# The first head group's weight columns split ahead of the rest, x loaded first, and item 0 waiting for its own copy

## What is computed

```python
q, kv = ln(x), ln(ctx)
qp, kp, vp = q @ Wq.T + bq, kv @ Wk.T + bk, kv @ Wv.T + bv
s = einsum(qh, kh) / sqrt(32) - scale[h] * dist(query_xy, token_xy) + offset[h]
s = where(token_mask, s, -inf)
x = x + (softmax(s) @ vh) @ Wo.T + bo
x = x + gelu(ln(x) @ W1.T + b1) @ W2.T + b2          # hidden width 2048
```

## Time and the profile before

| | |
|---|---|
| median of 3 runs | 1211.11 us (1210.51 to 1212.82) |
| the profiled execution | 1213.1 us, its span 1211.3 us |
| PE busy | 1189.5 us, 98% |
| POOL, DVE, ACT busy | 949.7, 908.5, 863.5 us |
| mean DMA rate | 193 GB/s |

### The profile page before, as it was taken

The page is one execution under the profiler, slowest core; times in us unless marked ns, Lnnn a source line. Parts: engine busy times, 40 slices in busy tenths (PEclk is TensorE's granted clock), DMA queues, the critical chain, the costliest instruction groups (busy, mean ns, idle before and its releaser), DMA issues.

```text
span 1211.3 us, 27819 instructions
## 1 busy us (share of the span) xinstructions
PE 1189.5 (98%) x9671; PEld 810.5 (67%) x9671; DVE 908.5 (75%) x2474; ACT 863.5 (71%) x1960; POOL 949.7 (78%) x1194
## 2 busy tenths in 40 slices
PE   7899999999999999999999999999999999999999
PEld 4466666667676766767676666767676676766666
DVE  6788868887787878778797887778787877668222
ACT  4699796868778786877778686877778687756332
POOL 5598988788798878889798878879787887758221
PEclk9899999999999999999999999999999999999999
DMA  8567768989799898989889897979988897867553
GB/s 256 168 174 220 176 166 185 212 175 235 179 213 211 188 212 190 222 172 236 196 189 214 194 211 177 233 178 201 222 185 213 191 217 159 190 168 171 148 149 104
DMA packets 434524, 233.23 MB, mean 193 GB/s; under 512 B 349888, under 2 KB 374864, under 8 KB 434384
## 3 DMA queue, kind: packets, MB, share of 16 engines
q1 hardware_dynamic: 434384, 231.45, 83.3%
HBM read 109.66 MB, written 12.58 MB: 101 GB/s over the span
## 4 chain that ended last, share of the span: by engine, by line
PE 88%; POOL 3%; DVE 3%; ACT 2%; issue 1%; SPq 1%; DMA 1%; DVEq 0%; POOLq 0%; ACTq 0%
PE ps_up L883 27%; PE ps_down L903 26%; PE ps_qk L790 12%; PE ps_vo L812 6%; PE ps_s L827 5%; PE ps_pv L868 3%; PE ps_pv L815 3%; PE ps_vo L815 3%; POOL soft L1592 1%; POOL soft L1611 1%; PE ps_down L931 1%; DVE soft L1372 1%; ACT soft L1071 0%; DMA xT<-x_nat 0%; PE ps_down L839 0%
## 5 line engine op out<-in xcount | busy, mean ns | idle before, releaser
L883 PE MATMUL ps_up<-hT,w 128*128 128x256 f16 x3072 | 377.0, 273 | 0.0
L1372 DVE CUSTOM_DVE_ANT_0 soft<-ps_s,soft,factor 128x256 f32<-128x256 f32 x512 | 226.1, 478 | 196.2 <-PE ps_s L827 196.2
L1071 ACT ACTIVATE soft<-soft,neg_max 128x256 f32<-128x256 f32 x512 | 255.7, 501 | 164.8 <-DVE neg_max L1372 163.6
L903 PE MATMUL ps_down<-w,hid 128*128 128x512 f16 x1476 | 359.6, 378 | 0.1
L883 PEld LDWEIGHTS ps_up<-hT,w 128*128 128x128 f16 x3072 | 300.6, 98 | 85.9
L1602 POOL TENSOR_SCALAR p_nat<-soft,row_inv 128x256 f16<-128x256 f32 x448 | 265.3, 603 | 71.2 <-DVE row_inv L1385 68.4
L1611 POOL TENSOR_SCALAR soft<-dist,scale_neg,offset 128x512 f32<-128x512 f32 x256 | 267.0, 1043 | 16.3 <-DVE p_nat L1391 15.4
L1391 DVE SCALAR_TENSOR_TENSOR p_nat<-soft,row_inv,p_nat 128x256 f16<-128x256 f32 x448 | 266.9, 635 | 0.8 <-POOL p_nat L1602 0.8
L1114 ACT ACTIVATE u<-ps_up,bias,up_scale 128x256 f32<-128x256 f32 x256 | 142.5, 557 | 127.1 <-PE ps_up L883 124.1
L903 PEld LDWEIGHTS ps_down<-w,hid 128*128 128x128 f16 x1476 | 141.6, 97 | 125.8 <-DVE x L1445 2.8
L1619 POOL TENSOR_SCALAR hid<-u,hid_scale 128x1024 f16<-128x1024 f32 x63 | 73.2, 1162 | 47.3 <-ACT u L1120 47.3
(11 more groups left out here) (166 smaller groups left out, 1548.4 us busy)
## 6 DMA issues: line engine op xcount, KB each, us to landing
w<-x_scratch SPq DMA_DIRECT2D x252, 256.0 KB, 3.1
stack<-qk_parts SPq DMA_DIRECT2D x256, 96.0 KB
raw<-in_ctx SPq DMA_DIRECT2D x32, 256.0 KB, 3.6
raw<-in_x SPq DMA_DIRECT2D x32, 256.0 KB, 4.2
c_stage<-in_w SPq DMA_DIRECT2D x16, 512.0 KB, 5.4
x<-in_x SPq DMA_DIRECT2D x32, 256.0 KB, 3.6
out<-x SPq DMA_DIRECT2D x31, 256.0 KB, 3.3
tok_rows<-in_tok_xy SPq DMA_DIRECT2D x16, 256.0 KB, 3.7
```

What stands on the lines that cost most here:

```text
L883: mm = e.matmul(ps_up[s % 2][:, 0:L], w_1_sb[:, wp, k, m * P:(m + 1) * P], hT[:, b % 2, :, xp * KT + k, :], start=(k, wp, xp) == (0, 0, 0) ...
L903: mm = e.matmul(ps_down[tt][:], left, w_2_sb[:, s % W2_RING, wp, :], start=first, stop=last)
L1071: e.activation(soft[:, ring, lc, :], soft[:, ring, lc, :], ACT.Exp, scale=-1.0, bias=neg_max[:, ring, lc:lc + 1], accum_out=row_sum[:, rin ...
L1372: e.tensor_tensor_reduce(soft[:, ring, lc, :], ps_s[:, lc * T:(lc + 1) * T], soft[:, ring, lc, :], factor[:, 0:1], 3.0e38, ALU.add, ALU.mi ...
```

## The change

It changes the order of the opening and of the first slots.

- x tiles 0 and 1 are loaded right behind ctx, ahead of W_k. They get a buffer of their own (`x_first`, in the place of `pT`), and ScalarE makes the high halves of all four tiles of batch 0 (`first_x_hi`).
- The small loads, tok_rows of batch 0 and W_v are issued by ScalarE.
- The first 128 columns of W_k and W_q (head group 0) are split first, by ScalarE and VectorE (`weight_hi_first`, `weight_lo_first`), and the projections of group 0 wait for each quarter of those alone. The other 384 columns are split by GpSimd and VectorE (`weight_hi_rest`, `weight_lo_rest`). Group 0's queries use the bank `ps_vo`, so they do not wait for the keys' low half.
- `keep_mask` comes after both halves of chunk 0, and both groups' mask rows follow it at once, ahead of the copies. Item 0 waits for its own copy and mask row (`s_head0`), items 1 to 3 for the other copies.
- W_v is split in slots 0 and 1, its bias matmuls are in slot 0, W_o's halves move from slots 1 and 2 to 2 and 3, W_1's and W_2's each two slots later. The Gram matmuls of W_o and of chunk 0 go from slot -2 to -1 and 1. Group 1 is projected in slots -2 and 0 (before -3 and -1), its copies are in slot 2 (before 1), batch 0's first value projection is in slot 2 (before 0), and `value_bias_out` is in slot 5 (before 4). The warming matmuls of slots -8 and -6 are 2 and 2 rather than 8 and 6.

```diff
@@ lists
-        CHUNK_AT = ((-6, -4), (-2, 0), (2, 4), (6, 8), (10, 12), (14, 16), (17, 19), (20, 22))
-        GRAM = (-31, -29, -6, -2, -2) + (2, 6, 10, 14, 18, 21, 24)
+        CHUNK_AT = ((-13, -12), (0, 2), (4, 6), (8, 10), (11, 13), (15, 17), (18, 20), (21, 23))
+        GRAM = (-31, -29, -4, -1, 1, 4, 8, 12, 16, 19, 22, 25)
...
-            return DMA * (HPG * (G // STACK_RING + 1) + G // HG + 1)
+            return DMA * (HPG * (G // STACK_RING + 1) + G // HG + 1 - (0 if G % STACK_RING else 2))
+        def qk_at(slot, first):
+            yield from (G for G in due(slot, first, GROUP, N_HG) if G != 1)
+            if slot == first + GROUP + 1:
+                yield 1
@@ SyncE
-                    e.dma_start(dst, src).then_inc(s_stack[ring], DMA)
+                    e.dma_start(dst, src).then_inc(s_head0 if G == 0 and j == 0 else s_stack[ring], DMA)
...
+            def mask_copy(G):
+                b, ring = G // HG, G % STACK_RING
+                gate.wait_ge(s_mkept, DMA)
+                src = mask_kept[b:b + 1, :].rearrange("p (o t) -> p o t", o=1).to_broadcast([1, HPG, T])
+                e.dma_start(stack[96:97, ring, :, 1 - query_side(G), :], src).then_inc(s_head0 if G == 0 else s_stack[ring], DMA)
...
-                for sec, at_slot in ((SEC_V, -25), (SEC_O, -14)):
+                for sec, at_slot in ((SEC_O, -14),):
...
-                if slot == -4:
+                if slot == -11:
                     keep_mask()
+                if slot == -10:
+                    for ring in range(STACK_RING):
+                        mask_copy(ring)
@@ TensorE
-                        gate.wait_ge(s_wlo, AT[sec] + 1)
+                        if G > 0:
+                            gate.wait_ge(s_wlo, AT[sec] + 1)
                         for k in range(KT):
+                            if G == 0:
+                                gate.wait_ge(s_wpart[sec], k + 1)
...
-                gate.wait_ge(s_stack[ring], n_stack(i // 4))
+                gate.wait_ge(*((s_head0, 2 * DMA) if i == 0 else (s_stack[ring], n_stack(i // 4))))
...
-                for at_slot, count in ((-30, 1), (-28, 1), (-8, 8), (-6, 6)):
+                for at_slot, count in ((-30, 1), (-28, 1), (-8, 2), (-6, 2)):
...
-                for sec, at_slot in ((SEC_K, -31), (SEC_Q, -29), (SEC_V, -3)):
+                for sec, at_slot in ((SEC_K, -29), (SEC_Q, -27), (SEC_V, 0)):
                     if slot == at_slot:
                         weight_bias(sec)
@@ ScalarE
+                if slot == -32:
+                    load_small()
+                for n in range(4):
+                    if slot == -30 + n:
+                        first_x_hi(n)
+                if slot == -27:
+                    load_value_weight()
...
-                for sec, at_slot in ((SEC_K, -25), (SEC_Q, -20), (SEC_V, -3)):
+                for sec, at_slot in ((SEC_K, -26), (SEC_Q, -20)):
                     if slot == at_slot:
-                        weight_hi(sec, range(KT))
-                for half_of in due(slot, 1, ITEM, 2):
+                        weight_hi_first(sec)
+                for half_of in due(slot, 0, ITEM, 2):
+                    weight_hi(SEC_V, range(2 * half_of, 2 * half_of + 2))
+                for half_of in due(slot, 2, ITEM, 2):
                     weight_hi(SEC_O, range(2 * half_of, 2 * half_of + 2))
-                if slot == -6:
+                if slot == -4:
                     dist_sqrt(0)
@@ VectorE
+            def weight_lo_first(sec, pieces):
+                for k in pieces:
+                    gate.wait_ge(s_fhi, KT * AT[sec] + k + 1)
+                    e.scalar_tensor_tensor(out=w_sec[sec][:, LO, k, 0:P], in0=w_stage[sec][:, k, 0:P], scalar=gain[:, sec, k:k + 1],
+                                           in1=w_sec[sec][:, HI, k, 0:P], op0=ALU.mult, op1=ALU.subtract).then_inc(s_wpart[sec])
...
+                for sec, pieces, at_slot in ((SEC_K, range(3), -6), (SEC_K, range(3, KT), -5), (SEC_Q, range(KT), -3)):
+                    if slot == at_slot:
+                        weight_lo_rest(sec, pieces)
@@ GpSimd
+            def weight_hi_rest(sec):
+                gate.wait_ge(s_gs, GAINED_Q if sec == SEC_Q else GS[AT[sec]])
+                for k in range(KT):
+                    e.tensor_scalar(w_sec[sec][:, HI, k, P:D], w_stage[sec][:, k, P:D], gain[:, sec, k:k + 1], 1.0, ALU.mult, ALU.mult).then_inc(s_rhi)
...
+                for sec, at_slot in ((SEC_K, -23), (SEC_Q, -21)):
+                    if slot == at_slot:
+                        weight_hi_rest(sec)
```

187 lines of the change are left out of this document (103 added, 84 removed).

## The result

The changed kernel took 1217.8 us, median of 4 runs (1217.15 to 1218.32), beside 1210.81 us for the kernel before (4 runs, 1210.25 to 1212.82): ratio 1.005, 95% interval 1.0038 to 1.0062. It is slower, by about 6 us, where I had forecast 1210.9 and a range up to 1214.2. The profiled execution took 1217.54 us with a span of 1215.5.

A forecast was written before the change was run, and what follows sets the result against it. TensorE was taken to bound the kernel, so the total moves with the first MLP matmul's start. First score -3.4, moved work +3.2, waits 0 gave -0.2 us: 1210.9 us, range 1205.8 to 1214.2.

The forecast's parts named there:

- term 1: Opening up to the first score: it comes at 30.9 us, 3.4 us sooner, with bounds 29.7 to 33.5.
- (d): Opening: keep_mask, issued on SyncE behind W_o and chunk 0, waits for them and lands at 27.2 us.
- (e): From keep_mask's landing to the first score: two mask copies, 1.4 us, then head 0's copy, 2.3 us.
- first rival: Opening: mask not held up, arithmetic decides; first score 8.3 us sooner at 26, total 1206 us; chance 0.22.
- step (c): Opening: W_v, W_o and chunk 0 load without a gap in 8.4 us, ending at 26.95.
- Step (a): Opening: small loads and tok_rows delay W_q's last quarter 0.8 us, to 13.35; W_k lands 1.4 to 2.2 us later.
- the opening gains nothing: Opening: transposes slowed beside W_v, or a copy of 3.74 us; first score 33.5, total 1213.5 us; chance 0.08.
- Term 2: Behind the first score: work moved there from the opening adds 3.2 us of TensorE time; waits cost the same.
- some 2 us: Slot 4: VectorE's 5 us of work makes score 6 wait this long, against 1.97 us ahead of score 4 before.
- TensorE's slot 0 has 5.6 us of work and covers it: Slots 0 and 1: VectorE ends slot 1 about 9.4 us after the first score, TensorE asks at 11.5.
- VectorE becomes the bound: Slots 0 to 5: two stalls of 2 us and a clock's fall of 1.7, +3.7, total 1214.6 us; chance 0.14.
- Slots 6 to 28 take other than 78.9 us: Sign that would prove the forecast wrong: the stretch up to the first MLP matmul departing from 78.9 us.

The follow-up runs named there:

- e2: Changed kernel with chunk 0 of W_1 loaded behind group 0's copies, so keep_mask has only W_o ahead of it; 1215.86 us, ratio 1.0031.
- e17: Kernel before with W_v asked for behind all of x's transposes; 1218.14 us, ratio 1.0053.
- e3: Changed kernel with the small loads and tok_rows on SyncE behind W_q and dist_square of part 0 two slots later; 1216.83 us, ratio 1.0043.
- e10: e5 with W_v asked for by SyncE behind the four transposes of x, ahead of W_o; 1213.45 us, ratio 1.001.
- e6: As e5, but four small loads (52 KB) left on ScalarE's queue, only tok_rows on SyncE; 1215.3 us, ratio 1.003.
- e5: Changed kernel with the edits of e2 and e3 together, q_neg's negation and dist_square five slots later than in e3; 1216.12 us, ratio 1.0035.
- e1: Kernel before run once more, no edit; 1212.09 us, ratio 0.9995.
- e12: Kernel before with only item 0's own copy wait and group 0's mask row copied ahead of the other copies; 1211.87 us, ratio 0.9997.
- e16: Kernel before with 18 more filler matmuls, 6 in each of slots 0, 1 and 2; 1213.67 us, ratio 1.0013.
- e18: Kernel before with the edits of e12 and e17 together; 1218.72 us, ratio 1.0056.
- e7: e5 with 2 fillers in place of 13 in slot 0; 1216.11 us, ratio 1.0035.
- e15: e14 with 2 fillers in place of 13 in slot 0; 1212.02 us, ratio 1.0001.
- e9: e7 with K's and Q's halves ahead of the exponentials and W_v's halves in slots 0 and 1; 1215.88 us, ratio 1.0025.
- e13: e10 with chunk 0 asked for behind the two ctx tiles of batch 1; 1213.78 us, ratio 1.0015.
- e4: Changed kernel with W_v's bias matmuls and both pairs of its halves back in the opening; 1219.32 us, ratio 1.0059.
- e14: e13 with norms and loads of W_1's chunks 5 to 7 in the slots of the kernel before; 1212.14 us, ratio 0.9998.

## Why the prediction was wrong

**The mechanism of term 1 was right, its end was 4.1 us off (30.9 forecast, 35.00 measured).** Steps (d) and (e) held: `keep_mask` waits for what is ahead of it in the queue (e2 took chunk 0 away: 3.06 us; in e17, where the loads ahead of it had landed, it took 1.8 us), two mask copies 1.34 (1.4 forecast), the copy 2.30 (2.3). By the rule weighed for the first rival (the Trainium skill, DMA: Bandwidth & Descriptors, "Queues, rings and completion order": completion is not first in, first out per issuing engine) the small mask might have passed the large loads. No run here shows that: the mask took 6.87 us, and 5.36, 7.05 and 7.18 in e2, e3 and e10. What failed is step (c), "All are issued before about 17.5, so the engines have no gap", for which no row was given and which had no bounds in the range. The last transpose was issued at 20.37 and W_o at 21.73. The windows of the changed kernel show where the DMA engines were idle or slow, and at the end the stretch that was at the forecast's rate, 0.70 us a quarter or 374 GB/s (columns as in rows 2; the last two are DMA share and GB/s):

```profile
4.50:6.50 2.00, 1.77 (x6) 0.98 (x4) 1.60 (x9) 0.00 (x0) 0.28 (x1) 1.00 0.73 135
14.50:15.80 1.30, 1.30 (x22) 1.02 (x26) 0.72 (x2) 1.30 (x3) 0.46 (x1) 1.00 0.21 53
...
22.40:24.40 2.00, 1.25 (x9) 0.59 (x6) 1.93 (x10) 2.00 (x7) 0.23 (x1) 1.00 1.05 70
25.00:30.40 5.40, 3.16 (x35) 2.82 (x36) 5.40 (x11) 2.60 (x3) 3.57 (x5) 1.00 1.04 376
```

From 22.40 to 24.40, right behind the last transpose's issue, the engines were busy (share 1.05) and moved 70 GB/s, and only from 25.00 on W_o and chunk 0 at 376. Three causes:
- Step (a) priced the small loads on ScalarE's queue at 0.8 us and their bytes. From 4.5 to 6.5 us the engines moved 135 GB/s, and 367 in the kernel before. There W_k's last quarter was used at 8.45 (the line below, PEld of the kernel before), so that 1.4 to 2.2 us later would be 9.9 to 10.7; it was used at about 13.3. Without the small loads it came at 9.76 (e3), as forecast; with 52 KB of them left, at about 12.5 (e6).
- That made VectorE and ScalarE, which work through their lists in order, late with x's second pair (17.27). I had counted x's path in DMA time alone. From 14.5 to 15.8 the DMA engines had little to do (share 0.21). That this follows from the late loads is read from the chain; in e5, which has neither the late W_k nor the late q_neg, SyncE began the second pair at 13.42, 3.3 us sooner than here.
- W_v's load, beside the transposes, made them slow to issue: 2.9 us in e5 against e10. Here the pairs took 4.24 and 5.00. By the rule that I had quoted for step (c) (the Trainium skill, DMA: Bandwidth & Descriptors, "Issuing engines are not separate DMA queues"), W_v on another queue takes nothing out of the way. The trace agrees: W_v on ScalarE's queue held up SyncE's transposes (6.40 us against 3.50). It cost 1.9 us more than its bytes, since in e10 the same bytes still lie ahead of the mask. The rival "the opening gains nothing" had named this mechanism, with a chance of 0.08 and the first score at 33.5, still too early.

```profile
8.45 0.11 PEld L695 LDWEIGHTS ps_down<-w_stage,cols 128*1 128x1 f32 x8 [0.32 <-DMA w_stage<-in_w_qkv]
```

**Term 2 had the right amount of work; its price was wrong in slots 4 and 5.** I forecast 3.2 us of TensorE work. Up to score 7 there were 255 matmuls instead of 188, and busy time rose by 29.91 - 27.57 = 2.3 against the profile of before and by 3.6 against e1, the stage by 1.9 and 3.8. The two profiles of the kernel before differ there by the granted clock: 0.89 over 29.54 us gives up 3.2 us, 0.94 over e1's 27.64 1.7, and the changed kernel's 0.95 over 31.46 1.6 (estimates from the windows). Up to score 5 the changed kernel took 19.51 us, within what the kernel before took (18.00 in e1, 19.90). From score 5 to score 7 it took 11.95, and 9.64 in the kernel before and all its variants (e1, e12, e16 to e18). These are the windows of slot 4 and slot 5, the kernel before first, the changed one below:

```profile
54.21:60.15 5.94, 5.94 (x31) 3.07 (x30) 3.69 (x11) 2.30 (x6) 4.53 (x7) 1.00 0.41 89
60.15:63.85 3.70, 3.70 (x33) 2.42 (x32) 3.10 (x10) 2.15 (x6) 3.40 (x5) 1.00 1.03 193
```

```profile
54.51:59.21 4.70, 3.48 (x37) 2.19 (x37) 4.53 (x20) 3.45 (x11) 3.54 (x5) 1.00 0.00 0
59.21:66.46 7.25, 7.25 (x43) 4.16 (x44) 3.98 (x13) 3.44 (x10) 4.64 (x7) 1.00 0.80 141
```

Before, TensorE is busy through both. After, it has 3.48 us of work in slot 4 while VectorE is busy for 4.53 of 4.70, and score 6 waits 1.22 us for a maximum. The prediction had this wait ("some 2 us") and set the wait ahead of score 4, which did go, against it. It had `value_bias_out` (3.60 us of matmuls) move from slot 4 to 5 "at the same price", and that is where the price lies: in slot 4 these matmuls stood beside VectorE's work, in slot 5 they are added to 3.65 us of TensorE's own. The rest is the Gram group of W_1's chunk 1 (1.08 us), which came from slot 2 to slot 4, where no filler is left to make room for it. TensorE's work rose by 10.73 - 9.64 = 1.09 and the wait is 1.22, together the 2.3 us. All fourteen changed kernels have it (11.55 to 11.95), so no experiment touched it; that the old slots would save it is read from these windows and was not tried.

In the kernel before added work costs about half of what it takes, since it first fills waits (e16). In the changed kernel taking 2.4 us out of slot 0 gained nothing (e7, e15): a wait of 3.4 to 3.5 us for VectorE's low half stood in its place. Nor did easing VectorE's list (e9, e13). "TensorE's slot 0 has 5.6 us of work and covers it" was right, and I read from these four that two chains of nearly the same length lie beside each other ahead of score 5. The rival "VectorE becomes the bound" was wrong as I priced it: the changed kernel has one wait of 1.22 us and one of 0.29 in these slots. Only e4 took work from both chains, and it put W_v's halves right ahead of item 0's maximum; what would shorten the slots ahead of score 5 stays open.

**The step I left out.** "Slots 6 to 28 take other than 78.9 us" was on my list of what would prove me wrong, and they took 79.87. The diff moves the norms of W_1's last chunks a slot later. I costed chunk 0's Gram matrix and passed over these. The waits ahead of two of the last scores grew from 1.15 and 0.30 to 1.76 and 1.31, and e14 got 0.97 us of this stage back.

**Sum.** Forecast -3.4 + 3.2. Measured +0.7 and +1.9, then +1.0 and +0.6 that I didn't have. With the opening mended (e10) and the norms put back (e14) the change is worth nothing: 0.9998 (0.9989 to 1.0007). So term 1 was attainable (28.97 to 30.19), and the stage behind it takes it back: 111.04 after the first score in e14 against 106.8 to 108.6 in e1, before and e12. Of the 2.5 us between e14 and e12, 2.0 lie in slots 4 and 5 (11.68 against 9.64) and 0.4 behind score 7. No version beat the kernel before. Of the 0.6 us behind the first MLP matmul I tried nothing; from there to the end all changed kernels took 1069.0 to 1069.6, the kernel before and its variants 1068.4 to 1068.9.

## What to carry to other kernels

Work that runs under a wait is free only as long as the wait is there; a change that brings the first useful step forward moves that work behind it, so price both together and ask which engines' chains are then of one length. Work of one engine that runs beside another's long list has no fixed price: moved by one slot, it leaves a wait behind and lengthens the slot that it comes to. When transfers are reordered, follow the order on every engine that consumes them, VectorE's and TensorE's lists too, and not the bytes alone. Go through every number in a schedule that the diff shifts, also where it shifts by one slot a hundred microseconds away.
